# A decoder layer on one core: the decay in k's bank, buffers of their own for the residuals, a new order, and x added to the first residual by an accumulating DMA

## The reference

```python
h0 = layernorm(x)                                 # the RWKV block works on h0 and has residuals of its own
h = layer_norm(h0); hh = time_shift(h)
xk, xv, xr = (h * tm + hh * (1 - tm) for tm in (att_tmk, att_tmv, att_tmr))
k, v, sr = xk @ Wk.T, xv @ Wv.T, sigmoid(xr @ Wr.T)
# wkv, one step in time, numerically stable: carry aa, bb, pp; w = -exp(time_decay)
ww = u + k_t; qq = maximum(pp, ww)
y = (exp(pp - qq) * aa + exp(ww - qq) * v_t) / (exp(pp - qq) * bb + exp(ww - qq))
ww2 = pp + w; qq2 = maximum(ww2, k_t)
aa, bb, pp = exp(ww2 - qq2) * aa + exp(k_t - qq2) * v_t, exp(ww2 - qq2) * bb + exp(k_t - qq2), qq2
h1 = h0 + (sr * y) @ Wo.T                         # first residual
h = layer_norm(h1)                                # and mixed with time_shift(h) again
h2 = h1 + sigmoid(xr @ Wrec.T) * (square(relu(xk @ Wkey.T)) @ Wval.T)
x2 = x + h2
x3 = x2 + attention(q=norm(x2), k=ctx, v=ctx)     # 16 x 16 heads of one token, causal over heads
out = x3 + (gelu((norm(x3) @ U1) @ V1 + b1) @ U2) @ V2 + b2
```

## Time and profile before

| | us |
|---|---|
| median of 3 runs | 1297.85 (1295.64 to 1297.94) |
| the profiled execution | 1296.42 |
| its span, first to last instruction | 1294.5 |
| busy: TensorE / VectorE / ScalarE / GpSimd | 1041.9 / 1076.4 / 972.5 / 870.2 |
| mean granted clock of TensorE, share of full | 0.933 |

### The profile page before, as it was taken

One profiled execution on the slowest core, in us unless ns is written; L12 is line 12 of the kernel. 1 busy time (PEld: TensorE's weight loads), 2 busy tenths in 40 slices (PEclk: granted clock), 3 DMA queues, 4 the chain that ended last, 5 costly groups with the idle time before them and its releaser, 6 DMA issues.

```text
span 1294.5 us, 14561 instructions
## 1 busy us (share of the span) xinstructions
PE 1041.9 (80%) x3584; PEld 586.1 (45%) x3584; DVE 1076.4 (83%) x2172; ACT 972.5 (75%) x2026; POOL 870.2 (67%) x783
## 2 busy tenths in 40 slices
PE   0569596979889697979889797979989797969625
PEld 0236263544536263644636263543637263545302
DVE  2673999998989899998989899999989889858681
ACT  7767678878777778877787778877787877656424
POOL 0110897959586777958686776949686877868590
PEclk9879799999989899999999899999999998979767
DMA  5010010101010010101010010101010000110000
GB/s 179 17 33 16 17 33 16 34 16 50 17 49 1 17 49 16 49 17 49 16 49 0 17 49 16 49 17 49 16 34 16 27 24 16 33 33 17 1 16 17
DMA packets 38964, 38.39 MB, mean 30 GB/s; under 512 B 2932, under 2 KB 38648, under 8 KB 38904
## 3 DMA queue, kind: packets, MB, share of 16 engines
q1 hardware_dynamic: 38904, 37.77, 9.2%
HBM read 29.38 MB, written 8.39 MB: 29 GB/s over the span
## 4 chain that ended last, share of the span: by engine, by line
PE 53%; DVE 23%; ACT 10%; issue 6%; POOL 5%; SPq 1%; DMA 1%; DVEq 0%; ACTq 0%; POOLq 0%
PE bank L795 17%; PE bank L848 15%; PE bank L879 4%; PE bank L872 4%; PE bank L802 4%; PE bank L863 4%; DVE aa L1242 4%; POOL prod L349 3%; DVE stat L1131 3%; ACT n L449 2%; DVE pp L1199 2%; PE bank L891 2%; POOL prod L337 2%; DVE x L1347 1%; DVE o_att L1333 1%
## 5 line engine op out<-in xcount | busy, mean ns | idle before, releaser
L337 POOL TENSOR_TENSOR prod<-q,kv_ctx 128x256 f32<-128x256 f32 (+5 forms) x448 | 370.1, 870 | 223.7 <-ACT q L449 223.7
L349 POOL TENSOR_TENSOR prod<-prob,v_dh 128x256 f32<-128x256 f32 (+3 forms) x256 | 399.1, 1599 | 36.0 <-ACT prob L551 36.0
L795 PE MATMUL bank<-xk,w_key 128*128 128x512 f32 x512 | 236.0, 606 | 16.5 <-DVE xk L1173 16.5
L848 PE MATMUL bank<-w_val,hidden 128*128 128x256 f32 x1024 | 223.6, 379 | 0.0
L848 PEld LDWEIGHTS bank<-w_val,hidden 128*128 128x128 f32 x1024 | 194.6, 190 | 26.5
L1333 DVE TENSOR_REDUCE o_att<-prod 128x64 f32<-128x256 f32 (+3 forms) x256 | 191.1, 807 | 7.8 <-POOL prod L349 7.7
L1301 DVE TENSOR_REDUCE score<-prod 128x16 f32<-128x256 f32 (+5 forms) x448 | 175.8, 466 | 8.7 <-POOL prod L337 8.7
L809 PE MATMUL bank<-ident,n 128*128 128x128 f32 x384 | 58.3, 294 | 126.7 <-ACT n L449 126.7
L795 PEld LDWEIGHTS bank<-xk,w_key 128*128 128x128 f32 x512 | 95.1, 193 | 138.5 <-issue 124.8
L357 POOL TENSOR_TENSOR rr<-rr,bb 128x512 f32<-128x512 f32 x32 | 42.4, 1324 | 129.8 <-DVE bb L1231 129.8
L809 PEld LDWEIGHTS bank<-ident,n 128*128 128x128 f32 x384 | 47.5, 151 | 160.4 <-issue 159.0
(11 more groups left out here) (100 smaller groups left out, 2026.9 us busy)
## 6 DMA issues: line engine op xcount, KB each, us to landing
x_in<-in_x SPq DMA_DIRECT2D x16, 512.0 KB, 3.5
kv_ctx<-in_ctx SPq DMA_DIRECT2D x16, 512.0 KB, 3.8
n<-in_x SPq DMA_DIRECT2D x16, 512.0 KB, 3.5
out<-y_out SPq DMA_DIRECT2D x16, 512.0 KB, 4.5
w_key<-in_wkey SPq DMA_DIRECT2D x1, 1024.0 KB
w_val<-in_wval SPq DMA_DIRECT2D x1, 1024.0 KB
w_k<-in_wk SPq DMA_DIRECT2D x1, 256.0 KB, 2.7
w_v<-in_wv SPq DMA_DIRECT2D x1, 256.0 KB, 3.1
```

Source lines behind the costliest of these rows:

```text
L337: ins = pool.tensor_tensor(o, a, b, ALU.mult)
L349: ins = pool.tensor_tensor(o, ph[:, HB * n:HB * n + HB, 0:keys].unsqueeze(2).to_broadcast(shape), vh[:, :, 0:keys].unsqueeze(1).to_broadca ...
L795: mm = pe.matmul(to[:, :], w[:, fi, P * f:P * f + P], src[:, fi, :], start=(fi == 0), stop=(fi == CH - 1))
L848: mm = pe.matmul(bank[6 + t // 2][:, C * (t % 2):C * (t % 2) + C], hidden[:, j, P * t:P * t + P], w_val[:, j, :], start=(j == 0), stop=(j ...
```

## The change

1. **The decay in k's bank.** e1 is gone. `split_rise` and `exp_e1` write to `bank[f]`, where k was, and both scans read it there. `project_r(f)`, which overwrites the bank, waits for the scans.
2. **x added by DMA.** `load_x_again`, `add_x_again`, `x_again` and `res_done` are gone. GpSimd issues a DMA from HBM to x1 with an accumulating operation; `second_residual` waits for it.
3. **Buffers.** x1 and x3 are two each, n4 has its own, o_att is x3.
4. **The halving of the denominator.** `ln_den` takes the factor 2 that `inverse_den` took as a bias.
5. **SP.** x(0) is issued ahead of the weights; the context of a group is loaded two steps later. TensorE waits for the weights at their first use.
6. **Table loads** only where the set changes: in a step of the loop there are now six.
7. **The order** of the stages within each engine's step is a new one, and the step starts at another point of it.

```diff
-        e1, e2, rr = (sb(n, [P, CH, W]) for n in ("e1", "e2", "rr"))
+        e2, rr = (sb(n, [P, CH, W]) for n in ("e2", "rr"))
-        x1 = sb("x1", [P, TT, C])
+        x1 = [sb(f"x1_{p}", [P, TT, C]) for p in range(2)]
-        o_att = sb("o_att", [P, TT * NH, HD])
-        x3 = sb("x3", [P, TT, C])
-
-        n4 = n2
+        x3 = [sb(f"x3_{p}", [P, TT, C]) for p in range(2)]
+
+        n4 = sb("n4", [P, TT, C])
...
+            sp.dma_start(x_in[:, :, :], x_g[0]).then_inc(x_loaded, 16)
             sp.dma_start(vec[:, :], vecs).then_inc(vec_loaded, 16)
...
-            def load_x_again(g, par):
-                sp.wait_ge(x1_done, upto(g, 2))
-                sp.dma_start(n1[par][:, :, :], x_g[g]).then_inc(x_again, 16)
...
+            def add_x(g, par):
+
+                pool.wait_ge(n2_done, upto(g, 1))
+                pool.wait_ge(stats_read[2], upto(g, 2))
+                if some(g):
+                    pool.wait_ge(x_added, 16 * g)
+                pool.dma_start(x1[par][:, :, :], x_g[g], accum_op=ALU.add).then_inc(x_added, 16)
...
-                act.activation(e1[:, f, :], rr[:, f, :], ACT.Relu)
+                act.activation(bank[f][:, :], rr[:, f, :], ACT.Relu)
...
-                act.activation(e1[:, f, :], e1[:, f, :], ACT.Exp, scale=-1.0).then_inc(e1_exp, 1)
+                act.activation(bank[f][:, :], bank[f][:, :], ACT.Exp, scale=-1.0).then_inc(e1_exp, 1)
...
-            pe.wait_ge(att_w_loaded, 16 * 3)
-            pe.wait_ge(rest_w_loaded, REST_W)
...
                 if on(1):
-                    pe.wait_ge(rise_done, upto(i - 1, 2, 1))
+                    pe.wait_ge(aa_done, upto(i - 1, 2, 1))
                     project_r(i - 1, 0)
...
+                if on(1):
+                    pe.wait_ge(bb_done, upto(i - 1, 2))
                     project_r(i - 1, 1)
...
-                    ins = dve.tensor_tensor_scan(aa[:, SEQ * f + s, 1:T + 1], e1[:, f, cols],
+                    ins = dve.tensor_tensor_scan(aa[:, SEQ * f + s, 1:T + 1], bank[f][:, cols],
...
-            def add_x_again(g, par):
-                dve.wait_ge(x_again, 16 * (g + 1))
-                dve.wait_ge(n2_done, upto(g, 1))
-                dve.tensor_tensor(x1[:, :, :], x1[:, :, :], n1[par][:, :, :], ALU.add).then_inc(res_done, 1)
...
-                dve.wait_ge(res_done, upto(g, 1))
+                dve.wait_ge(x_added, 16 * (g + 1))
```

More of the change, by code:

```diff
@@ new lines, in step @@
+                if on(4):
+                    sum_values(i - 4, p, 1, 2)
+                if on(0):
+                    mean_1(i)
+                if on(4):
+                    inverse_mass(i - 4, 1)
+                    over_mass(i - 4, p, 0)
+                    sum_values(i - 4, p, 2, 0)
+                if on(1):
+                    att_before_r(i - 1, 0)
+                    att_before_k(i - 1, 0)
+                    att_before_k(i - 1, 1)
+                if on(3):
+                    gate_values(i - 3, 0)
+                    second_residual(i - 3, 1 - p, 0)
@@ new lines, in step @@
+                if on(4):
+                    third_residual(i - 4, p, 0)
+                if on(1):
+                    att_before_v(i - 1, 0)
+                if on(3):
+                    stats_3(i - 3, 1 - p, 0)
+                if on(4):
+                    sum_values(i - 4, p, 3, 1)
+                    over_mass(i - 4, p, 1)
+                if on(3):
+                    gate_values(i - 3, 1)
+                    second_residual(i - 3, 1 - p, 1)
+                    stats_3(i - 3, 1 - p, 1)
+                    mean_3(i - 3)
@@ new lines, in step @@
+                if on(2):
+                    divide_num(i - 2, 1)
+                if on(1):
+                    scan_pp(i - 1, 0)
+                if on(4):
+                    stats_4(i - 4, p, 0)
+                    third_residual(i - 4, p, 1)
+                if on(1):
+                    rise(i - 1, 0)
+                if on(4):
+                    stats_4(i - 4, p, 1)
+                    mean_4(i - 4)
+                if on(1):
+                    att_before_v(i - 1, 1)
+                    scan_pp(i - 1, 1)
```

648 lines of the change are left out of this document (313 added, 335 removed).

## The result

The changed kernel takes **1336.28 us** (median of four runs, 1332.49 to 1345.64) where the kernel before takes 1296.74 on the same chip: a ratio of 1.032, 95% interval 1.026 to 1.039. It is slower by 40 us. The forecast was 1261 us, so it is 75 us above it, and the sign is wrong.

The account below looks back on a forecast made before the run. It took a chain handed between TensorE and VectorE as the bound: 40.4 + 27.9 + 1.9 = 70.2 us, with jump and clock 71.0 against 72.9. Fill -9, early spacings -3, steps -23, drain -2 gave 1261 us, range 1236 to 1297.

Parts of the forecast that it names:

- TensorE's side: Part of a step from project_u1 to gate_values, forecast at 40.4 us with a hand-over of 0.1.
- VectorE's side: Part of a step from gate_values to the end of the second half's bb scans, forecast at 27.9 us.
- the jump: Loop jump at the start of VectorE's step: of 2.5 us, 0.8 left every second step, +0.4 us a step.
- the clock: TensorE at its lower clock after idling: part of a slow project_u1's 1.6 us is paid, +0.4 us a step.
- third_residual now lies beside busy GpSimd, +0.5: Term between gate_values and the end of the bb scans: third_residual slowed beside GpSimd, 0.5 us more.
- 12.9 us of work to gate_values: VectorE's work from last_residual to gate_values, against TensorE's 14.6 us, so VectorE would be 1.7 us early.
- Rival (b): DMA late, second_residual waits: mild, 1261 to 1297, chance 0.07; severe, slower than before, 1321 at 14 us, chance 0.14.
- The accumulating DMA: GpSimd's DMA adding x into x1: 7 us, twice the plain load, hidden within 9.7 us free before second_residual.
- add_x_again: Removed VectorE addition of x: 16 instructions of 1365 ns, 1.36 us a step.
- The decay: Decay moved to k's bank: scans at most 2.5 us less a step; aa pair 2.18 to 1.33, -0.85, in the sum.
- ScalarE's table loads: Six table loads a step instead of four, 2.6 us more on ScalarE, costed at nothing where off the path.
- The fill: Start of the kernel: x(0) loaded first, so project_k(0) starts at about 24 instead of 33.08, -9 us.

Follow-up runs that it names:

- gap: The changed kernel with one more wait: GpSimd, behind its DMA issue, waits for over_mass's first half before the values' last tile; 1262.4 us, 0.975.
- dma_last: The changed kernel with the accumulating DMA issued behind the last tile of GpSimd's values instead of ahead of it; 1325.7 us, 1.023.
- no_dma: The changed kernel without the accumulating DMA, so x is missing from the first residual, over_mass in its early place; 1259.9 us, 0.974.
- plain_dma: The changed kernel with GpSimd's DMA at its place as a plain load into an unused buffer, x not added; 1320.1 us, 1.020.
- sp_dma: The changed kernel with the DMA replaced by SyncE's plain load into an unused buffer, GpSimd issuing none, x not added; 1267.0 us, 0.977.
- mass_late_no_dma: mass_late without the accumulating DMA, so x is not added to the first residual; 1276.7 us, 0.989.
- dma_early_mass_late: The changed kernel with the DMA issued ahead of all value products, and the first half's over_mass and third_residual behind the last values; 1316.1 us, 1.017.
- mass_late: The changed kernel with the first half's over_mass and third_residual moved behind the sums of the last value tile; 1271.5 us, 0.984.

## Why the prediction was wrong

**What bounds the kernel, and the cut of the period: right.** gap is the changed kernel without over_mass's shut-out, and it can be read by the forecast's own sum. TensorE's side, project_u1 to gate_values: 607.11 - 566.73 = 40.4 us, forecast 40.4. VectorE's side to the end of the bb scans: 634.33 - 607.11 = 27.2, forecast 27.9. To the next project_u1: 637.01 - 634.33 = 2.7, forecast 1.9. Together 70.3 against 70.2, and the time is 1262.4 against 1261. So close a hit is in part luck: this step is one of the short ones. Over ten steps the parts are 41.4, 27.4 and 2.5 in the mean, 71.3 together (three of the ten, in which shift_scores is held, have 42.6 to 45.5 us in TensorE's part), and y_out comes every 71.6 us, against 71.0 forecast with the jump and the clock. In the changed kernel the three parts are 635.25 - 591.23 = 44.0, then 28.9 and 3.6 (project_u1 follows at 667.67), 76.4 together. Of the 6.2 us between the two steps 3.6 are in TensorE's part, where over_mass lies; 1.7 and 0.9 are in the other two, where project_o takes 3.75 us and the halves of project_r 3.22 and 3.68 us, at a granted clock of 0.56 (660 to 667 us).

**The step that failed** stands in "VectorE side": "third_residual now lies beside busy GpSimd, +0.5", and with it in the jump's "12.9 us of work to gate_values". I looked there for what the new order brings beside GpSimd, priced one instruction and only in the part between gate_values and the scans. over_mass(A, 0), with two operands in SBUF as well, lies in the other part, which I took from the old list as TensorE's alone, with VectorE 1.7 us early. It needed 5.1 us more, 3.6 of them on the path, and divide_num(D, 0), in the same part, takes 2.0 us instead of 0.65: from 615.94 to 635.25 VectorE needed 19.3 us where the forecast had 12.9. Even if I had seen it I would have priced it wrongly: the aa scan's 2.18 and 3.20 us would have given 1 to 2 us, no row showed 5.8 in the loop (the trace of before has a single one, in the drain, which I show in the last section), and the cause was a thing that I had weighed for its landing alone. Rival (b) held the DMA responsible for the slower side, by lateness; the sign was there with a chance of 0.14, the mechanism was not.

**The accumulating DMA:** 7 us taken, 5.9 measured, and hidden as forecast. 9.7 us from issue to use, 607.94 - 597.23 = 10.7 in gap; dma_last shows that the room is real and what lies behind it. "The engines that move data are 10% busy" and "descriptors are made by GpSimd itself" were both looked at for the transfer's own time. What GpSimd's issuing does to VectorE was not asked.

**add_x_again:** 1.36 us a step, 22 us, forecast; 14 to 17 us measured.

**The decay:** the scans' time came as forecast (0.67). Its worth was mis-sized: -0.85 us a step in the sum, because the cut of before held one pair of aa scans and gave a wait of no price; the runs show 43 to 58 us gross and 12 us for the wait. The two are not quite the same quantity: the forecast priced the move in the old stretch, the runs price it in the new order, where four pairs of scans stand ahead of project_r. That VectorE's side came out only 0.5 to 0.7 us too high is in part luck.

**The Trainium skill's rule** (SBUF — State Buffer, Who interferes with whom) that VectorE's instructions with two operands in SBUF contend with GpSimd's and those with one do not, is borne out here: over_mass, shift_scores and divide_num were held, and the scans with one operand in a bank were not (674 and 669 ns). The same page (SBUF: two separate sides) says that whoever starts first holds the pair of ports for the whole of its instruction. That would make the wait that of one GpSimd instruction. Over_mass in no_dma agrees with that (at most 1.5 us, beside value products of 1.6); over_mass in the changed kernel doesn't, nor does shift_scores at 1056.19 in no_dma (5.68 us): the wait lasted until a whole run of instructions was over.

**ScalarE's table loads:** 100 instead of 89, busy time 974.0 against 972.5. TensorE waits for the gelus ahead of project_u2 for 0.2 us at a time in the loop; one wait of 7.9 us stands in the drain. At nothing in the loop, as forecast. **The jump:** its gap on VectorE is 1.3 to 1.6 us instead of 2.5, forecast 0.8. **The fill:** -9 forecast, first project_k at 24.79 (forecast "about 24"), -8.0 to -9.7 measured. **The clock:** +0.4 a step forecast; in the changed kernel project_o pays 1.9 us a step for the idle time ahead of it, which gap does not (3.78 and 1.97 us).

## What to carry to other kernels

When an instruction is moved to stand beside another engine's stream, price every instruction of the stretch that reads two operands from SBUF, not only the one that the eye is on, and take the worst row of such a meeting for the upper end. A DMA issued from a compute engine's queue costs more than its landing: look at what other engines do beside the run of instructions around the issue, and try the issue by another queue or one wait that breaks the run at the right place (here one wait on GpSimd gave back 74 us). A kernel that takes one suspect out while all else stays in its place (no_dma) told more in one run than the three in which things were moved.

## What the runs showed of the hardware

- VectorE's instruction with two operands in SBUF can be kept out not for one instruction of GpSimd but until GpSimd's stream ends, 5.3 to 6.2 us in the loop. It happened to the first half's over_mass behind a DMA issued by GpSimd, whether accumulating or plain: 13 of 16 in the changed kernel and 13 of 16 in plain_dma, all that start 0.7 to 2.3 us into the stream behind the issue. It happened in none of the 16 of no_dma and of sp_dma (at most 1.5 and 2.3 us).
- It isn't bound to a DMA. shift_scores is held in the same way in kernels in which GpSimd issues none: once in no_dma (1056.19 us), at 281.88 and 570.54 in sp_dma, at 426.71 and 924.80 in mass_late_no_dma. From sp_dma, VectorE and GpSimd; the stream ends at 574.94, VectorE's instruction at 575.49:

```profile
570.54 4.95 DVE L1347 TENSOR_TENSOR prob<-score,top 128x512 f32<-128x512 f32 x1
```

```profile
563.72 11.22 POOL L337 TENSOR_TENSOR prod<-q,kv_ctx 128x256 f32<-128x256 f32 x14
```

- The kernel before shows one in the drain, where GpSimd's stream has no DMA issue (VectorE, then GpSimd; the stream ends at 1234.71, VectorE's instruction at 1235.26):

```profile
1227.14 8.12 DVE L1314 TENSOR_TENSOR prob<-score,top 128x512 f32<-128x512 f32 x1
```

```profile
1212.42 22.29 POOL L337 TENSOR_TENSOR prod<-q,kv_ctx 128x256 f32<-128x256 f32 x28 [12.98 <-ACT q L449]
```

- At which of GpSimd's instruction boundaries VectorE is let in stays open. An issue ahead of the stream (the changed kernel), one behind it (dma_early_mass_late) and none (the rows above) all occur with it, and an issue behind it also occurs without it (dma_last). How far into the stream VectorE starts doesn't decide it alone: in no_dma shift_scores starts 6.10 us behind the first of 14 score products both at 985.18 and at 1056.19, and takes 0.75 and 5.68 us. No run here held everything but the phase of the two streams constant, and none tells the issue itself from its transfer in flight beside the stream.
- An accumulating DMA of 512 KB issued by GpSimd lands after 5.9 us and occupies GpSimd's queue for 1.3; the plain one 3.9 and 0.79. SyncE's issue of the plain load landed after 5.8 us at its own, other time of the step.
- Waits of 5.5 to 6.5 us in the loop of the changed kernel left TensorE at the lower clock for the projection that followed (3.8 us instead of 1.9, granted clock 0.50). Behind waits of 1.7 to 2.0 us in gap it took 1.96 to 1.99 us, once 2.51; behind waits of 2.2 us in mass_late it took from 2.5 to 3.7 us.
